# RK4 stages on two PSUM banks in turn, in a GRU, attention, oscillator and gated-FFN kernel

## What is computed

```python
def _derivative(q, p, drive, coupling, bias):
    i_couple = jnp.tanh(q) @ coupling.T
    dq = q - q ** 3 / 3.0 - p + drive + i_couple + bias
    dp = EPSILON * (q + ALPHA - BETA * p)
    return (dq, dp)

def _rk4_step(q, p, drive, coupling, bias):
    dq1, dp1 = _derivative(q, p, drive, coupling, bias)
    dq2, dp2 = _derivative(q + 0.5 * DT * dq1, p + 0.5 * DT * dp1, drive, coupling, bias)
    dq3, dp3 = _derivative(q + 0.5 * DT * dq2, p + 0.5 * DT * dp2, drive, coupling, bias)
    dq4, dp4 = _derivative(q + DT * dq3, p + DT * dp3, drive, coupling, bias)
...
gate = jax.nn.silu(bitlinear(x, w_gate))
up = bitlinear(x, w_up)
return bitlinear(gate * up, w_down)
```

## Time and profile before

| | us |
|---|---|
| median of 3 runs | 603.66 (603.34 to 605.01) |
| the profiled execution | 605.59 |
| its span in the profile | 603.6 |
| the oscillator loop within the span | 297 to 590 |
| DVE busy, PE busy (whole span) | 504.7 (84%), 571.7 (95%) |
| ACT busy, POOL busy (whole span) | 393.1 (65%), 254.8 (42%) |

### The profile page before, as it was taken

How to read it: one execution, slowest core, us unless ns; L and a number is a source line. 1 busy time by engine, 2 the same in 40 slices (tenths; PEclk the granted TensorE clock), 3 DMA queues, 4 the chain that set the end, 5 groups by cost and what they waited for, 6 DMA issues and landing times.

```text
span 603.6 us, 15678 instructions
## 1 busy us (share of the span) xinstructions
PE 571.7 (95%) x5692; PEld 521.2 (86%) x5692; DVE 504.7 (84%) x1483; ACT 393.1 (65%) x959; POOL 254.8 (42%) x401
## 2 busy tenths in 40 slices
PE   9999999999999988999988999999999999999997
PEld 8999999999999887888877888788788788888885
DVE  3777777676777768999989999999999999999996
ACT  3545454454544453464557888888888888888885
POOL 0433323233232264231154556556556555555550
PEclk9999999999999998999999999999999999999999
DMA  8500000000000000500000000000000000000001
GB/s 260 185 2 2 1 1 2 1 1 2 2 1 1 19 3 2 189 4 3 1 1 1 11 19 18 12 19 18 11 19 19 9 21 13 16 19 10 19 17 37
DMA packets 12523, 14.97 MB, mean 25 GB/s; under 512 B 1632, under 2 KB 10144, under 8 KB 12448
## 3 DMA queue, kind: packets, MB, share of 16 engines
q1 hardware_dynamic: 12448, 13.97, 6.8%
HBM read 9.78 MB, written 4.19 MB: 23 GB/s over the span
## 4 chain that ended last, share of the span: by engine, by line
PE 74%; DVE 18%; issue 4%; ACT 3%; DVEq 0%; POOL 0%; ACTq 0%; POOLq 0%
PE PS L463 22%; PE PS L315 18%; PE PS L338 13%; PE PS L562 4%; PE PS L438 4%; PE PS L515 3%; PE PS L536 3%; DVE q_s L1096 3%; DVE h_s L1076 3%; DVE big L958 2%; PE PS L398 2%; DVE q_s L1113 2%; PE PS L321 2%; DVE PS L1050 1%; PE PS L553 1%
## 5 line engine op out<-in xcount | busy, mean ns | idle before, releaser
L463 PE MATMUL PS<-k_s,h_s 128*128 128x128 f32 x1024 | 159.4, 283 | 15.7 <-DVE PS L1050 13.3
L463 PEld LDWEIGHTS PS<-k_s,h_s 128*128 128x128 f32 x1024 | 131.8, 191 | 32.2 <-DVE PS L1050 19.3
L315 PE MATMUL PS<-part 128*128 128x256 f32 x900 | 115.6, 286 | 0.0
L315 PEld LDWEIGHTS PS<-part 128*128 128x128 f32 x900 | 109.8, 191 | 0.0
L758 ACT ACTIVATE k_s<-h_s 128x128 f32<-128x128 f32 x256 | 71.9, 307 | 48.2 <-DVE h_s L1076 30.4
L338 PE MATMUL PS<-big,wrk 128*128 128x128 f32 x744 | 88.4, 275 | 1.7 <-DVE big L916 1.7
L338 PEld LDWEIGHTS PS<-big,wrk 128*128 128x128 f32 x744 | 85.8, 192 | 2.3 <-DVE big L916 2.3
L1236 POOL COPY h_s<-big 128x256 f32<-128x256 f32 x32 | 21.5, 671 | 129.6 <-DVE big L916 129.6
L463 PE MATMUL PS<-h_s 128*128 128x128 f32 x384 | 74.2, 275 | 0.0
L463 PEld LDWEIGHTS PS<-h_s 128*128 128x128 f32 x384 | 58.3, 192 | 0.0
L652 ACT ACTIVATE big<-big 128x256 f32<-128x256 f32 x32 | 13.3, 416 | 63.2 <-DVE big L898 63.2
(11 more groups left out here) (188 smaller groups left out, 1232.4 us busy)
## 6 DMA issues: line engine op xcount, KB each, us to landing
out<-q_s SPq DMA_DIRECT2D x32, 128.0 KB, 1.7
x_s<-in_xT SPq DMA_DIRECT2D x14, 256.0 KB, 6.0
k_s<-in_wgT SPq DMA_DIRECT2D x1, 832.0 KB, 5.5
k_s<-in_wuT SPq DMA_DIRECT2D x1, 832.0 KB, 7.2
k_s<-in_wih SPq DMA_DIRECT2D x3, 256.0 KB, 4.5
wrk<-in_whh SPq DMA_DIRECT2D x3, 256.0 KB, 4.5
h_s<-in_wdT SPq DMA_DIRECT2D x1, 768.0 KB, 6.7
x_s<-in_xT SPq DMA_DIRECT2D x4, 128.0 KB, 3.7
```

Of the source, the lines that this page charges most:

```text
L315: r = pe.matmul(p, y, x, start=i == 0, stop=i == len(passes) - 1)
L463: return pe.matmul(PS[:, m, 0:128], w, x, start=False, stop=True, skip_group_check=True)
```

## The change

The stages take turns on two banks: stage `slot` has both halves in bank `slot % 2`.

- DVE writes each seed as one instruction of 128x256. `seed_2` of step t follows `seed_1` at the head of the step, `seed_3` stands after the first `nexts`, `seed_4` after the second, and `seed_1` of the next step after `last_next`: each one stage earlier than before.
- PE has a new function `linear`, which does the identity products of the next stage right after the coupling products of the present one. `coupled` takes k outside and m inside and signals once for both halves.
- DVE's `t2` is behind `seed_3`, `t3` no longer waits for a state, and `cubic` of the fourth stage is behind `t4`.
- POOL's order becomes u3, W3, v1, t1, uz, WZ, dq, ob, next p. W3's wait for `t2` and WZ's wait for `seed_3` are gone. POOL has as many instructions as before; DVE has four seeds a step in the place of eight.

The diff, cut to its core:

```diff
+        stage_bank = lambda slot: PS[:, slot % 2, 0:256]
...
-            def add(m, w, x):
-                return pe.matmul(PS[:, m, 0:128], w, x, start=False, stop=True, skip_group_check=True)
-            def coupled(slot, scale=None, x=None):
+            def add(slot, m, w, x):
+                return pe.matmul(cm(stage_bank(slot), m), w, x, start=False, stop=True, skip_group_check=True)
+            def linear(slot, scale, x):
+                pe.wait_ge(s_seed, slot + 1)
+                if slot % 4 > 1:
+                    pe.wait_ge(s_next, q_next(slot // 4, slot % 4 - 2, 1))
                 for m in range(2):
-                    pe.wait_ge(s_seed, 2 * slot + m + 1)
-                    pe.wait_ge(s_th, 2 * slot + 1)
-                    add(m, coupU[:, 0, m * 128:(m + 1) * 128], cm(th[slot % 2], 0))
-                    pe.wait_ge(s_th, 2 * slot + 2)
-                    r = add(m, coupU[:, 1, m * 128:(m + 1) * 128], cm(th[slot % 2], 1))
-                    if x is not None:
-                        r = add(m, scale, cm(x, m))
-                    r.then_inc(s_ps, 1)
+                    add(slot, m, scale, cm(x, m))
+            def coupled(slot):
+                pe.wait_ge(s_seed, slot + 1)
+                for k in range(2):
+                    pe.wait_ge(s_th, 2 * slot + k + 1)
+                    for m in range(2):
+                        r = add(slot, m, coupU[:, k, m * 128:(m + 1) * 128], cm(th[slot % 2], k))
+                r.then_inc(s_ps, 1)
...
                 coupled(4 * t)
                 if t == 0:
                     keep_warm(7, 3)
+                linear(4 * t + 1, id_q1, qn[t % 2])
...
-                coupled(4 * t + 1, id_q1, qn[t % 2])
+                coupled(4 * t + 1)
...
+                linear(4 * t + 2, id_s2, qs[0])
...
+                linear(4 * t + 3, id_z3, qs[1])
...
             def seed_1(t):
                 if t:
                     ve.wait_ge(s_p, t)
+                    ve.wait_ge(s_next, q_next(t - 1, 2, 1))
                 else:
                     ve.wait_ge(s_add, 16)
                 ve.wait_ge(s_dr, drive_done(t))
-                for m in range(2):
-                    if t:
-                        ve.wait_ge(s_q, 2 * t - 1 + m)
-                    ve.scalar_tensor_tensor(PS[:, m, 0:128], cm(pn[t % 2], m), -1 / lam, I_at(t)[:, m], ALU.mult,
-                                            ALU.add).then_inc(s_seed, 1)
-            def seed_2(t, m):
-                ve.wait_ge(s_next, q_next(t, 0, m))
-                ve.scalar_tensor_tensor(PS[:, m, 0:128], cm(pn[t % 2], m), -(1 - A) / lam, I_at(t)[:, m], ALU.mult,
+                ve.scalar_tensor_tensor(two(stage_bank(0)), two(pn[t % 2]), -1 / lam, I_at(t), ALU.mult,
                                         ALU.add).then_inc(s_seed, 1)
-            def seed_3(t, m):
+            def seed_2(t):
+                if t:
+                    ve.wait_ge(s_q, 2 * t)
+                ve.scalar_tensor_tensor(two(stage_bank(1)), two(pn[t % 2]), -(1 - A) / lam, I_at(t), ALU.mult,
+                                        ALU.add).then_inc(s_seed, 1)
+            def seed_3(t):
                 ve.wait_ge(s_W3, t + 1)
-                ve.wait_ge(s_next, q_next(t, 1, m))
-                ve.scalar_tensor_tensor(PS[:, m, 0:128], cm(qn[t % 2], m), (1 + 2 * A * kap) / 6, cm(W3, m),
-                                        ALU.mult, ALU.add).then_inc(s_seed, 1)
+                ve.wait_ge(s_next, q_next(t, 0, 1))
+                ve.scalar_tensor_tensor(stage_bank(2), qn[t % 2], (1 + 2 * A * kap) / 6, W3, ALU.mult,
+                                        ALU.add).then_inc(s_seed, 1)
             def seed_4(t):
                 ve.wait_ge(s_dq, t + 1)
                 ve.wait_ge(s_WZ, t + 1)
-                for m in range(2):
-                    ve.wait_ge(s_next, q_next(t, 2, m))
-                    ve.scalar_tensor_tensor(PS[:, m, 0:128], cm(dq, m), 1 / 3, cm(WZ, m), ALU.mult,
-                                            ALU.add).then_inc(s_seed, 1)
+                ve.wait_ge(s_next, q_next(t, 1, 1))
+                ve.scalar_tensor_tensor(stage_bank(3), dq, 1 / 3, WZ, ALU.mult, ALU.add).then_inc(s_seed, 1)
...
             def nexts(slot, dst):
                 ve.wait_ge(s_w, slot + 1)
+                ve.wait_ge(s_ps, slot + 1)
                 for m in range(2):
-                    ve.wait_ge(s_ps, 2 * slot + m + 1)
-                    ve.scalar_tensor_tensor(dst(m), PS[:, m, 0:128], of_ps[slot % 4], cm(w_, m), ALU.mult,
+                    ve.scalar_tensor_tensor(cm(dst, m), cm(stage_bank(slot), m), of_ps[slot % 4], cm(w_, m), ALU.mult,
                                             ALU.add if slot % 4 == 2 else ALU.subtract).then_inc(s_next, 1)
...
-                seed_1(t)
+                seed_2(t)
...
-                nexts(4 * t, lambda m: cm(qs[0], m))
-                seed_2(t, 0)
-                if t < T - 1:
-                    ve.wait_ge(s_t1, t + 1)
-                    ve.wait_ge(s_next, q_next(t, 0, 1))
-                    ve.scalar_tensor_tensor(t2, t1, horner[1], qs[0], ALU.mult, ALU.add).then_inc(s_t2, 1)
+                nexts(4 * t, qs[0])
+
                 if t >= 1:
                     ve.wait_ge(s_red, t)
                     if t == 1:
                         ve.wait_ge(s_wvec, 3)
                     ve.scalar_tensor_tensor(q_at(i, 1, 3), wide(q_at(i, 0), 3), TINY * lam, wvec[:, 0:3], ALU.max,
                                             ALU.mult).then_inc(s_tq, 1)
-                seed_2(t, 1)
+                seed_3(t)
                 if t >= 1:
                     ve.wait_ge(s_tq, t)
                     ve.reciprocal(q_at(t - 1, 4), q_at(t - 1, 1)).then_inc(s_s1, 1)
+                if t < T - 1:
+                    ve.wait_ge(s_t1, t + 1)
+                    ve.scalar_tensor_tensor(t2, t1, horner[1], qs[0], ALU.mult, ALU.add).then_inc(s_t2, 1)
...
-                nexts(4 * t + 1, lambda m: cm(qs[1], m))
-                seed_3(t, 0)
-                seed_3(t, 1)
+                nexts(4 * t + 1, qs[1])
+
+                seed_4(t)
...
-                nexts(4 * t + 2, lambda m: cm(qs[2], m))
-                seed_4(t)
+                nexts(4 * t + 2, qs[2])
+
                 if t >= 2:
                     ve.wait_ge(s_mxh, i + 1)
                     ve.scalar_tensor_tensor(h_at(i, 1, 2), wide(h_at(i, 0), 2), TINY, wvec[:, 3:5], ALU.max,
                                             ALU.mult).then_inc(s_thh, 1)
                 if t < T - 1:
                     ve.wait_ge(s_t2, t + 1)
-                    ve.wait_ge(s_next, q_next(t, 1, 1))
                     ve.scalar_tensor_tensor(t3, t2, horner[2], qs[1], ALU.mult, ALU.add).then_inc(s_t3, 1)
-                cubic(4 * t + 3, qs[2])
+                if t >= 2:
+                    ve.wait_ge(s_thh, i + 1)
+                    ve.reciprocal(h_at(i, 4), h_at(i, 1)).then_inc(s_s2, 1)
                 if t < T - 1:
                     ve.wait_ge(s_t3, t + 1)
                     ve.wait_ge(s_next, q_next(t, 2, 1))
                     ve.scalar_tensor_tensor(t4, t3, horner[3], qs[2], ALU.mult, ALU.subtract).then_inc(s_t4, 1)
-                if t >= 2:
-                    ve.wait_ge(s_thh, i + 1)
-                    ve.reciprocal(h_at(i, 4), h_at(i, 1)).then_inc(s_s2, 1)
+                cubic(4 * t + 3, qs[2])
                 last_next(t)
+                if t < T - 1:
+                    seed_1(t + 1)
...
-                    po_.wait_ge(s_seed, 8 * t + 2)
+                    po_.wait_ge(s_seed, 4 * t + 1)
+                po_.tensor_scalar(u3, p, -n2 / lam, 0.0, ALU.mult, ALU.add).then_inc(s_u3, 1)
+                po_.wait_ge(s_dr, drive_done(t))
+                po_.wait_ge(s_u3, t + 1)
+                po_.tensor_tensor(two(W3), two(u3), I_at(t), ALU.add).then_inc(s_W3, 1)
                 if t < T - 1:
                     po_.tensor_scalar(v1, p, horner[0], 0.0, ALU.mult, ALU.add).then_inc(s_v1, 1)
                     po_.wait_ge(s_v1, t + 1)
                     po_.tensor_tensor(t1, v1, q, ALU.add).then_inc(s_t1, 1)
                 po_.tensor_scalar(uz, p, -n3 / lam, 0.0, ALU.mult, ALU.add).then_inc(s_uz, 1)
-                po_.tensor_scalar(u3, p, -n2 / lam, 0.0, ALU.mult, ALU.add).then_inc(s_u3, 1)
-                if t < T - 1:
-                    po_.wait_ge(s_t2, t + 1)
-                else:
-                    po_.wait_ge(s_seed, 8 * t + 4)
-                po_.wait_ge(s_dr, drive_done(t))
-                po_.wait_ge(s_u3, t + 1)
-                po_.tensor_tensor(two(W3), two(u3), I_at(t), ALU.add).then_inc(s_W3, 1)
+                po_.wait_ge(s_uz, t + 1)
+                po_.tensor_tensor(two(WZ), two(uz), I_at(t), ALU.add).then_inc(s_WZ, 1)
+                po_.wait_ge(s_next, q_next(t, 0, 1))
+                po_.tensor_tensor(dq, qs[0], q, ALU.subtract).then_inc(s_dq, 1)
                 if t >= 4:
                     i = t - 4
                     po_.wait_ge(s_x1k, i + 1)
```

(5 more changed lines are left out.)

13 lines of the change are left out of this document (7 added, 6 removed).

## The result

| | before | after |
|---|---|---|
| median | 603.78 us (4 runs, 603.34 to 605.01) | 631.96 us (4 runs, 631.16 to 632.59) |
| profiled execution | 605.59 | 631.16 |
| its span | 603.6 | 629.2 |

The ratio is 1.046, with a 95% interval from 1.044 to 1.048. The change makes the kernel slower, as I forecast, but by 28.2 us where I had said 18.4. The time lies 2 us above the range.

A forecast was written before the change was run, and what follows sets the result against it. DVE and PE were taken as close to full, with POOL's chain coming to the front: 9.81 us a step for 9.13, +18.4 us in total on the median of 603.66, forecast 622 us, range 606 to 630.

The forecast's parts named there:

- The holds: How long an instruction blocks the other engine: one-input POOL 0.27 us, two-input POOL 0.58, whole seed or `t2` on DVE 0.28.
- the small scale instruction: DVE, behind the first `nexts`, two SBUF operands: it and `seed_3` were to wait for POOL's t1, about 0.46 us.
- POOL's chain: POOL from the end of `seed_1` through dq: 4.49 us without blocking plus 0.35 of blocks, 4.84 us.
- The sum: Whole loop: 0.68 us for 27 steps, +0.3 for two early steps, -0.3 at the end, total +18.4 us.
- steps 0 and 1: Start of the loop: the first gains some 0.5 us, the second loses about as much at the weight rounding; net 0.
- The fourth stage: Third `nexts` to `last_next`, over tanh and eight PE passes with signals of 0.04: 1.87 us.
- if PE's clock leaves 1.00 in its longer pauses: PE's granted clock: a condition that would make the forecast wrong at the root; the rows of before gave no sign.
- Steps 2 and 3: Early loop, before ob exists: without `seed_4`'s 0.52 us block, +0.16 us each, +0.3 together.
- the last step: End of the loop: it has no v1, t1, t2 to t4, so -0.3 us.
- Rival 1: DVE and POOL: no block of weight, stages get shorter, step 8.94 us, 598 us, faster; chance 0.11.
- Rival 3: Waits only moved: blocking and the gained bank cancel, step stays 9.13, 604 us; needs hold below 0.27; chance 0.05.
- Rival 2: `seed_4` wins against POOL's ob, the 0.52 us falls away, 608 us; chance 0.22 with short holds beside it.

## Why the prediction was right in sign and short in size

**The cause was right.** It predicted that POOL, freed of its waits, meets DVE's seeds, and that this outweighs the shorter stages. Taking out the waits alone costs 30 us on the old kernel. Keeping ob away gives back 11.6 us, and taking the second SBUF operand from the seeds 20.6 us. With POOL's work shaped around the seeds, and `t2` moved, the same banks and early products are 0.7% faster than the kernel before.

**The holds.** I had 0.58 us for a POOL instruction with two inputs and 0.27 for one. Measured with 0.43 as a seed's own length: `seed_4` behind ob 0.18 + 0.40 = 0.58, `seed_3` behind t1 0.01 + 0.58 = 0.59, in the kernel before without waits 0.05 + 0.55 = 0.60; with one input 0.25 (`seed_4` behind ob) and 0.27 (`t2` behind uz, in the run with seeds from PSUM). The Trainium skill (SBUF — State Buffer, section "Who interferes with whom") has the block last until the other instruction is finished, which by the prediction's working was 10.2 us a step. The measured step of 10.00 looks halfway to that, and 631.96 us is near the 633 that the prediction put beside it (its range ended at 630), but the experiments show the holds at their short length; the rest has another source. Why a hold ends before the profile's end of the instruction is open; POOL's next instruction starts 0.69 us after a two-input one that is given 0.72.

**Where the block fell.** I had it at the small scale instruction (0.46). It escaped: 448.66, before t1 at 448.84; `seed_3`, 0.01 behind t1, took it whole (0.58), and then held uz (0.58 long for 0.41; I had 0.65). This shift costs nothing in the loop: POOL's chain, from the end of `seed_1` (446.80) to WZ at 450.19 and dq's end, 0.73 + 0.72 later, is 4.84 us, the figure predicted, though the blocks in it lie elsewhere than I had them, which is in part luck. From dq's end (441.65) to the maximum (442.55) it is 0.90 for 0.89, the maximum 0.93, the cubic 0.44 for 0.45, `last_next` and `seed_1` 0.83.

**The terms that were mis-sized** are two. The sum had +18.4 us for the loop; measured in the traces it is +27.9. Of the 9.5 between them 5.1 are the fourth stage, 27 times, and 4.1 are steps 0 and 1.

*The fourth stage*: "third `nexts` to `last_next` 1.87 as above". It measured 2.05. The loop with it is 4.84 + 0.90 + 0.93 + 0.44 + 2.05 + 0.83 = 9.99, the 10.00 seen. I had taken every signal for 0.04. Two of the three in this stage go to an instruction whose late wait is the last written: PE's starts 0.09 later, of which its passes give back 0.03, and `last_next` 0.10. With these waits first the stage measured 1.88 and the step 9.83, against 1.87 and 9.81 predicted.

*Steps 0 and 1*, which I had put at nothing: "step 0 has POOL's work done ahead and gains some 0.5, step 1 loses about as much". Step 0 lost 1.6 us. In the kernel before v1, t1, uz and u3 are done by 292.34, ahead of the loop; in the new order only u3 is, since the second instruction, W3, waits for the drive. It starts at 294.40, 0.02 ahead of `seed_1`, which takes 0.99, and the rest of POOL's work follows beside the seeds, `t2` and the rounding. With the seeds' second operand from PSUM step 0 takes 8.59. Step 1 lost 2.6: with the clock up it takes 10.11 for 9.18, with `seed_3` at 1.01 and a rounding at 1.15 that took 0.60 before, and the fall of the clock adds 1.65, of which step 2 gives back 0.8. I had named "if PE's clock leaves 1.00 in its longer pauses" as what would make me wrong. It did, once in this trace, and costs 0.8 us net; that the pause was the cause is not shown.

**The rest.** Steps 2 and 3 cost 0.7 for the 0.3 said, and the last step with what follows saved 0.5 for 0.3. The span was missed by 7.2 us only (629.2 for 622.0), since the untouched part was 2.3 us shorter in this trace. I took off 1.9 us because the profiled execution of before lay that far above its median; its clock fell ahead of the loop, as the rows above show, so that was right to do. The median was missed by 9.9 us, 0.4 more than the 9.5 of the loop, which is less than the scatter of either kernel's executions.

**Rivals.** Rival 1 (no block) is out: seeds of 1.01 and 0.83, and 620.4 us with ob kept away. Rival 3 (hold below 0.27, 604 us) is out with the holds of 0.58. Rival 2 (`seed_4` wins against ob) would have ob at 1.0 us; it has 0.72, since `seed_4` came 0.18 behind, not 0.07. Part of that is again the late wait written last: next state at 441.67, `seed_4` at 441.80, and with the order turned round this gap was 0.03. The block was 0.40 for 0.52 accordingly, and the end came at the same time.

## What to carry to other kernels

A wait on an engine with time to spare may be what keeps it out of another's way. Before it is taken out, write down which instructions of the two will then run at once, and which of them have two SBUF operands; better, put the idle engine's two-input work where the other reads PSUM. Add up a loop with measured signals, each for its own kind of wait. And add up the first steps from rows too, instruction by instruction: here two steps of 32, put at nothing, were 4 of the 9.5 us missed. Before a run is taken for the proof of a cause, see whether the effect also comes and goes between runs that don't touch it.

## What the runs showed of the hardware

- The block between POOL and DVE ends before the profile's end of the instruction that holds it: 0.58 to 0.60 us into a two-input 128x256 POOL instruction of 0.73, 0.25 to 0.27 into a one-input one of 0.41. A DVE instruction of three columns is held for as long (0.68 for 0.15) as a large one. With one of its two operands from PSUM, DVE wasn't held at all (0.43 with t1 and ob running). But the rounding of the weights, one SBUF operand to bf16, was held as well (1.14 for 0.59 behind W3).
- The order in which an instruction's waits are written has a price. If the late one is written first, the instruction starts 0.03 to 0.05 us after its signaller's end, if last, 0.10 to 0.14. This showed on DVE in both directions and on PE in one. That it is the order and not the semaphore is supported by `nexts`, where the same reversal made the gap larger (0.03 to 0.10).
- The clock of PE fell to the 1.2 GHz level for 3 to 4 us in some executions and not in others of the same code: behind the pause in step 1 (1.67 us in the changed kernel, fall; 1.67 with ob waiting, none; 1.68 with one input for ob, fall), and ahead of the loop (2.03 us before 231.35 in the kernel before, fall; 2.12 before 231.06 with ob waiting, none). The fall ahead of the loop costs 1.5 us, that in step 1 0.8 net. Later in the loop of the changed kernel PE waits for up to 0.6 us for a tanh, and the clock stays at 1.00.
